# Attention of layer 3: score products on 64-row halves of the array, stacks loaded without stages, causal zeros set after the exponential, maxima over pairs of heads

## What is computed

```python
qkv = jnp.einsum('bsm,qhkm->qbhsk', x, w_qkv)          # x: layer-normed input
scores = jnp.einsum('bhqk,bhsk->bhqs', Q, K) / jnp.sqrt(jnp.float32(d_k))
scores = jnp.where(causal, -jnp.inf, scores)            # causal: key after query
probs = jax.nn.softmax(scores, axis=-1)
attn = jnp.einsum('bhqs,bhsk->bhqk', probs, V)          # then w_o, layer norm, x = x + ...
```

## Time and profile before

| | |
|---|---|
| median of 3 runs | 1885.78 us (1883.0 to 1894.48) |
| profiled execution | 1892.21 us, of which the span is 1890.4 us |
| layers 1 and 2, to the barrier near 395 us | 395 us |
| layer 3, from there to the barrier near 1190 us | about 795 us |
| layer 4 with its weight loads | about 700 us |
| mean granted TensorE clock | 0.932 of 2.4 GHz |
| busy: PE, DVE, ACT, POOL | 1648.1, 1080.8, 914.3, 279.1 us |

### The profile page before, as it was taken

The page is one execution under the profiler, slowest core; times in us unless marked ns, Lnnn a source line. Parts: engine busy times, 40 slices in busy tenths (PEclk is TensorE's granted clock), DMA queues, the critical chain, the costliest instruction groups (busy, mean ns, idle before and its releaser), DMA issues.

```text
span 1890.4 us, 25225 instructions
## 1 busy us (share of the span) xinstructions
PE 1648.1 (87%) x9170; PEld 1214.8 (64%) x9170; DVE 1080.8 (57%) x3056; ACT 914.3 (48%) x1750; POOL 279.1 (15%) x729
## 2 busy tenths in 40 slices
PE   6998857625998999899989998399999999999996
PEld 5877755523555555555545554288888888888885
DVE  5867548855975787678767872234333343434332
ACT  3454425622465666566656666134343443434432
POOL 2123221230110121012101201200101011010101
PEclk9999977866799999999999999599999999999998
DMA  3001112225422531363054400540000000000000
GB/s 117 12 34 36 44 40 89 76 76 66 54 27 35 80 68 25 43 83 69 13 61 54 82 11 2 174 143 1 1 23 23 1 23 1 23 16 8 12 1 23
DMA packets 52869, 83.39 MB, mean 44 GB/s; under 512 B 6784, under 2 KB 41216, under 8 KB 49856
## 3 DMA queue, kind: packets, MB, share of 16 engines
q1 hardware_dynamic: 46416, 68.72, 18.7%
q0 software_dynamic: 5840, 12.33, 2.1%
q10 hardware_dynamic: 480, 0.66, 0.3%
HBM read 43.40 MB, written 12.58 MB: 30 GB/s over the span
## 4 chain that ended last, share of the span: by engine, by line
PE 64%; DVE 13%; SPq 6%; ACT 5%; DMA 5%; issue 4%; POOL 1%; POOLq 1%; ACTq 1%; DVEq 0%
PE psum L812 24%; PE psum L542 12%; PE psum L786 6%; SPq L1748 6%; PE psum L727 5%; PE psum L682 5%; PE psum L709 4%; PE psum L825 3%; PE psum L546 2%; DVE mxs L1416 2%; ACT pr L1027 2%; DMA stage_k<-k_lo 2%; DMA shared_xn<-x_stream 1%; PE psum L712 1%; DVE stat_out L1140 1%
## 5 line engine op out<-in xcount | busy, mean ns | idle before, releaser
L812 PE MATMUL psum<-fh_hi,fWh 128*128 128x512 f32 x1024 | 399.0, 390 | 0.0
L812 PE MATMUL psum<-fh_lo,fWh 128*128 128x512 f32 x1024 | 398.4, 389 | 0.0
L1027 ACT ACTIVATE pr<-psum 128x512 f32<-128x512 f32 (+3 forms) x768 | 344.4, 495 | 106.8 <-PE psum L712 76.4
L1176 DVE TENSOR_TENSOR fh_lo<-fraw,fh_hi 128x512 fp32r<-128x512 f32 x192 | 132.9, 692 | 380.3 <-ACT fh_hi L1090 335.6
L682 PE MATMUL psum<-Ks,Qs 128*128 128x512 f32 (+3 forms) x768 | 311.7, 423 | 33.6 <-DVE mxs L1416 13.2
L709 PE MATMUL psum<-Qs,Ks 128*128 128x512 f32 (+3 forms) x768 | 265.2, 361 | 29.4 <-ACT pr L1027 28.4
L1086 ACT ACTIVATE fraw<-psum,fsch 128x512 f32<-128x512 f32 x128 | 86.5, 676 | 301.9 <-PE psum L812 301.9
L812 PEld LDWEIGHTS psum<-fh_hi,fWh 128*128 128x128 f32 x1024 | 192.2, 188 | 39.7
L812 PEld LDWEIGHTS psum<-fh_lo,fWh 128*128 128x128 f32 x1024 | 192.3, 188 | 39.6
L682 PEld LDWEIGHTS psum<-Ks,Qs 128*128 128x128 f32 x768 | 156.5, 204 | 91.0 <-DVE mxs L1423 31.6
L709 PEld LDWEIGHTS psum<-Qs,Ks 128*128 128x128 f32 x768 | 147.2, 192 | 56.7 <-ACT pr L1027 47.6
(11 more groups left out here) (228 smaller groups left out, 2893.5 us busy)
## 6 DMA issues: line engine op xcount, KB each, us to landing
stage_q<-q_hi SPq DMA_DIRECT2D x60, 128.0 KB, 5.5
stage_k<-k_hi SPq DMA_DIRECT2D x60, 128.0 KB, 5.3
xr<-x_stream SPq DMA_DIRECT2D x9, 512.0 KB, 6.0
x<-in_x SPq DMA_DIRECT2D x8, 512.0 KB, 8.0
raw<-in_h1T SPq DMA_DIRECT2D x16, 256.0 KB, 2.6
raw<-in_h2T SPq DMA_DIRECT2D x16, 256.0 KB, 2.7
x_stream<-x SPq DMA_DIRECT2D x8, 512.0 KB, 3.2
shared_xn<-x_stream SPq DMA_DIRECT2D x8, 512.0 KB, 4.5
```

Source lines behind the costliest of these rows:

```text
L812: m = e.matmul(psum[:, ring4.bank[u], :], f.W[name][:, c, oc * P:(oc + 1) * P], h[:, c, :], start=(c, k) == (0, 0), stop=(c, k) == last)
L1027: e.activation(pr[:, 2 * (s % 2) + pair, side, 0:width], psum[:, (3, 4, 5)[nr % 3], 0:width], ACT.Exp, scale=SC1).then_inc(*mark("act", "s ...
L1176: return e.tensor_tensor(dst, src, plain(hi), ALU.subtract).then_inc(*mark("dve", kind))
```

## The change

Eight edits in layer 3, all in one diff:

1. `Ks` has one copy without zeros. `score3` (was `max3`) and `st3` take rows 64·side to 64·side + 48 (50), one half of the array's rows. Within a step a `score3` of one side alternates with an `st3` of the **other** side.
2. On the diagonal blocks of the maxima, a new PE unit `diag3` adds the bf16 triangle (two matmuls a pair of heads) behind all eight products of the step. DVE's custom instruction, `maskw` and its reading of the accumulator go.
3. DVE's `max3` is one reduce for both sides of a pair (two banks in one instruction, 128x2 out of up to 1024), 24 a group instead of 48; `best3` joins the two column halves of queries 512 to 1023.
4. The triangle products L712 of `st3` go; a new POOL unit `mask3` sets zeros in the first 128 columns of the four exponentials (one `affine_select` over 512 elements a row) on the 8 diagonal steps.
5. `pv3` runs two steps behind instead of one, and `pr` has three buffers instead of two.
6. The DMAs of `stack3` write `Qs` and `Ks` themselves. `copy3`, the stages and their memsets go; `NST` is 4. Later groups' `stack3` stand 36 (25 at a new batch) instead of 27 (23) steps ahead.
7. **Banks:** the ring of the loop has two places, `[0, 2]`. A pair's two scores take one place (banks 0 and 1, or 2 and 3), and so does every side unit. `st3` has 4, 5 and 6.
8. The order of `MAXBLOCKS` and some steps in `plan` differ (`val3` of the first half one step earlier, the second half's projection 3 to 4 steps earlier, the output projection 2 later).

```diff
-NST = 3
+NST = 4
...
-    (0, 0), (1, 0), (3, 0), (4, 0), (5, 0), (2, 0), (7, 0), (7, BANK), (6, 0), (6, BANK), (5, BANK), (4, BANK))]
+    (3, 0), (0, 0), (4, 0), (1, 0), (5, 0), (2, 0), (6, 0), (4, BANK), (7, 0), (5, BANK), (7, BANK), (6, BANK))]
...
-            at([s0 - (27 if g % G else 23)], [("stack3", g, None)])
...
+            at([max(s0 - (36 if g % G else 25), -LEAD)], [("stack3", g, None)])
...
-            at([s0 + n for n in (21, 22, 23, 24, 26, 27)], proj(b + 1, 1))
+            at([s0 + n for n in (18, 19, 20, 21, 22, 23)], proj(b + 1, 1))
...
         for pair, side in HEADS:
...
-                units.append(("max3", *divmod(s + LEAD, NS), pair, side))
+            if ahead:
+                products.append(("score3", *ahead, pair, side))
             if 0 <= s < total:
-                units.append(("st3", s, pair, side))
...
+                products.append(("st3", s, pair, 1 - side if ahead else side))
+        if ahead:
+            i, k0, width = MAXBLOCKS[ahead[1]]
+            diagonal = k0 + width == (i + 1) * P
+            units += [(kind, *ahead, pair) for kind in (("diag3", "max3") if diagonal else ("max3",)) for pair in range(2)]
...
+            units.append(("mask3", s))
+        if 0 <= s - 2 < total:
+            units.append(("pv3", s - 2))
...
-                ring3.banks, ring3.turn = [2], 0
+                ring3.banks, ring3.turn = [0, 2], 0
...
-            Ks = [sb(ph, f"Ks{i}", [P, 2, 2, S], f32r) for i in range(NST)]
-            stage = [sb(ph, f"stage_{m}", [P, 2, S]) for m in "qk"]
...
+            Ks = [sb(ph, f"Ks{i}", [P, 2, S], f32r) for i in range(NST)]
...
+            def score3(g, n, pair, side):
+                u, (i, k0, width), r = ("max3", g, n, pair), MAXBLOCKS[n], rows_of(side, KR)
+                w.wait_ge(*stacked(g))
+                w.wait_ge(*back(ring3, u))
+                e.matmul(psum[:, ring3.bank[u] + side, 0:width], Qs[g % NST][r, pair, i * P:(i + 1) * P],
...
+            def diag3(g, n, pair):
+                bank, width = ring3.bank["max3", g, n, pair], MAXBLOCKS[n][2]
+                for side in range(2):
+                    m = e.matmul(psum[:, bank + side, width - P:width], ident16[:, :], tri16[:, :], start=False, stop=True)
+                m.then_inc(*mark("pe", "diag3"))
...
-                if diag:
-                    m = e.matmul(psum[:, bank, 0:P], tri16[:, :], ident16[:, :], start=False, stop=True)
...
-                e.activation(Ks[g % NST][r, side, pair, :], stage[1][r, pair, :], ACT.Copy).then_inc(*mark("act", "copy3"))
...
+                e.tensor_reduce(mxs[:, g % 2, k0 // BANK, :, pair, i], psum[:, bank:bank + 2, 0:width], AX.X,
+                                ALU.max).then_inc(*mark("dve", "max3"))
...
+                e.affine_select(out=blocks, in_=blocks, compare_op=ALU.is_ge, fill=0.0, base=0, pattern=[[0, 2], [0, 2], [1, P]],
+                                channel_multiplier=-1).then_inc(*mark("pool", "mask3"))
```

213 lines of the change are left out of this document (76 added, 137 removed), and 2 rows, old and new, of the table hands_back.

## The result

The changed kernel takes 1984.86 us (median of 4 runs, 1974.34 to 1992.46), the kernel before beside it 1889.44 us: the ratio is 1.0503, with a 95% interval from 1.044 to 1.0566. It is 5% slower, where 1871 us was forecast and 1930 was the upper end of the range. The profiled execution lasts 1990.6 us against 1890.4, at a mean granted clock of 0.869 against 0.932. The layers 1, 2 and 4 are unchanged; the 100 us lie between 450 us and the loop's end at 1277 us (1177 before); what follows the loop is as long as it was.

A forecast was written before the change was run, and what follows sets the result against it. PE looked like the bound, with a bank chain setting a floor of 2.60 us per 512-wide step. 1892.2 - 12 (three batches) - 4 (start copies) + 1 (extra step) = 1877 profiled; median 6.4 lower: 1871 us, range 1792 to 1930.

The forecast's parts named there:

- Rival (c): PE's array streams about half the time; if the loop were granted 0.87, +45 us, 1916, slower; chance 0.20.
- The quiet group: Loop group with hardly a side unit: PE 31.3, DVE 3.0, side units 1.0, together 35.3 us against 35.6.
- a pair's reduce: DVE's maximum for both sides of a pair, not in the trace: between 1.05 and 1.26, taken as 1.15 us.
- the four triangles: `diag3` on 8 diagonal steps a group: 0.48 us for four, between 0.23 and 0.92; 3.8 us a group.
- 3.0 us for DVE: Added to a quiet group where DVE's step outlasts PE's: 0.9 + 0.3, 0.5 and 0.2 among its terms.
- The overlap: Score products on array halves run two at a time; without it, 2.2 us a group more.
- rival (b): The halves don't run at the same time: 2.2 us a group, +35, 1906 us, slower; chance 0.12.
- Side units: Sharing the maxima's two places, a `qk3` delays pair 1's scores: 2.2 instead of 1.61 us, +0.6 each.
- "No change" for the 17 steps ahead of the loop: Lead steps at half clock, DVE busy 32 of 38 us: fewer reduces but longer chains, taken as no change.
- The last two groups: End of the last batch, groups priced at 30.3 and 28.6 us; that batch 136 us, no change.
- The change of form: Tiling-mode changes drain PE; a diagonal step has three, not two: another 0.16 us 128 times would be 20 us, 1891.
- group 6 without its stage wait: Group 6 of the loop: 35.3 against 48.4 us, since two `val3` and the stage's DMA wait are gone.

The follow-up runs named there:

- e12: Changed kernel with triangles behind each pair, side units in the `st3` banks and score products over all 128 rows (two heads summed): 1866.8 us, ratio 0.9877.
- e1: Changed kernel with layer 3's score products over all 128 rows instead of 64-row halves (two heads summed): 1942.8 us, ratio 1.0301.
- e3: Changed kernel with each pair's triangles right behind that pair's two products instead of behind all four: 1901.4 us, ratio 1.009.
- e8: Changed kernel with score products over all 128 rows and triangles right behind each pair (two heads summed): 1890.3 us, ratio 1.0026.
- e10: Changed kernel, still with halves, with triangles right behind each pair and side units in the three `st3` banks: 1887.9 us, ratio 0.9975.

## Why the prediction was wrong

The table puts the runs side by side: rows of the products, place of the triangles, where the side units go, clock for 490 to 1180 us (the loop of e12 ends at 1153; its own clock is 0.99), groups 10 and 5 in us, and the median.

| kernel | rows | triangles | side units | clock | group 10 | group 5 | us |
|---|---|---|---|---|---|---|---|
| changed | half | behind all | places | 0.83 | 36.2 | 55.3 | 1985 |
| e1 | full | behind all | places | 0.98 | 37.5 | 55.2 | 1943 |
| e3 | half | by pairs | places | 0.89 | 33.2 | 49.5 | 1901 |
| e8 | full | by pairs | places | 0.99 | 34.8 | 52.0 | 1890 |
| e10 | half | by pairs | `st3` banks | 0.87 | 32.3 | 48.0 | 1888 |
| e12 | full | by pairs | `st3` banks | 0.97 | 33.9 | 49.2 | 1867 |

**The step that failed is the clock.** The sum priced every product at the full clock and put the clock itself at nothing. Rival (c) named it, with a chance of 0.20 and a price of 45 us at a clock of 0.87. It came at 0.83. Full rows take 42 us off (54 between the loops of the two profiled executions, 768 and 714 us) although they give up the overlap, which is worth 1.3 us in each of the 14 groups with both kinds of products. So the clock costs some 60 to 70 us here, an estimate; on the kernel before the halves cost 72 net. Rival (c)'s rate, 45 us for a fifth of the loop at the low level, fits this: against the kernel before a third more of the profiled loop is at it (mean clock 0.82 against 0.98). What was wrong was how much of the loop would run low, and why. I had derived it from the share of time in which the array streams and from a stretch in which PE idles; the run on rows 0 to 63 shows a clock of 0.50 with PE busy for 98% of the stretch. In these kernels it isn't a risk beside the halves, it is their price. The Trainium skill ("TensorE: Matmul & The Clock Gate", Part 1: The HAM clock gate) ties the clock to how busy the engine has been; that row doesn't agree, if busy is what the profile counts, and the measurement decides.

**The quiet group** was nearly right where the clock is high: 35.3 us forecast, 36.2 measured in group 10 at 0.95. Its terms: a pair's reduce 1.15 forecast, 1.18 measured (2.36 us for two at 512 columns); the four triangles 0.48 forecast, 0.32 from their weight load (1038.57) to that of `pv3` (1038.89). The forecast had 3.0 us for DVE, and the triangles by pairs gave back 3.0 (36.2 to 33.2). That the numbers agree is partly luck: by the forecast's own terms only 1.4 of its 3.0 lay on diagonal steps. So the price of the triangles' place was about twice what the sum had for it, and I left it in without asking what it would do to the clock.

**The overlap** was priced at 2.2 us a group in rival (b), and is worth 1.2 to 1.6 net where the clock is high. Rival (b) itself fell. The Trainium skill ("TensorEngine Tiling (Array Packing)", Key Properties) says that different tiles load and multiply in parallel; the row at 1027.83 agrees.

**Side units** were priced at +0.6 us each. Group 5 came out as forecast but for 2 us (53, against 55.2 at a clock of 1.00), groups 4 and 7 didn't: 48.3 and 41.0 forecast, 54.3 and 45.4 in the run with full rows at 0.97 and 1.00. Over three batches that is some 30 us. Two waits share this, which the run with side units in the `st3` banks and the triangles by pairs both shorten (49.4 and 42.5).

**The start and the end.** "No change" for the 17 steps ahead of the loop was wrong by 7 us (the loop begins at 509.1 us, not 502.3), and the low clock reaches into the loop, 0.62 in a stretch that had 1.00:

```profile
509.10:537.00 27.90, 25.99 (x138) 12.22 (x137) 13.82 (x20) 12.61 (x28) 3.86 (x7) 0.62 0.01 2
```

```profile
509.00:537.00 28.00, 26.92 (x171) 15.12 (x170) 21.40 (x78) 19.04 (x39) 6.22 (x18) 1.00 0.51 59
```

(the same stretch, changed and before). The last two groups were forecast at 59 us and take 77.5 at a clock of 0.67; with full rows (e1) they take 59.6.

So the clock isn't the whole miss. For the run with full rows (e1), 1871 forecast, + 18 for the overlap given up, + 30 for the groups with side units and + 13 for the start (515.2 us there) make 1932, against 1943 measured. Of the 11 us that are left, 5 are the step from the profiled execution to the median, 6.4 us in the forecast and 1.3 there (1944.1 and 1942.8); 6 stay open. The halves put 42 us more on top.

**The change of form.** The prediction weighed the Trainium skill's rule ("TensorEngine Tiling (Array Packing)", Key Properties) that a change of tiling mode drains TensorE, at 20 us for 128 diagonal steps, and left it out of its sum. The trace agrees with the rule for halves against full rows too. The last product of a 512-wide step and the first triangle behind it, with halves and with full rows (e1), both at full clock:

```profile
1034.81 0.49 PE L722 MATMUL psum<-Qs,Ks 50*128 50x512 f32 x1
1035.23 0.28 PE L703 MATMUL psum<-tri,ident 128*128 128x128 bf16 x2
```

```profile
1015.86 0.39 PE L722 MATMUL psum<-Qs,Ks 128*128 128x512 f32 x1
1016.09 0.28 PE L703 MATMUL psum<-tri,ident 128*128 128x128 bf16 x2
```

The starts are 0.42 us apart with halves and 0.23 with full rows: 0.19 us, as much as a change costs in the run with only the maxima in halves. On the 128 diagonal steps, where DVE waits for the triangles, that would be 24 us, so the rule's 20 us did come. In the sum they hardly show, by luck: with this wait in front the four triangles cost 0.19 + 0.32 = 0.51 us, and the forecast had 0.48. The 1.2 to 1.6 us that the overlap is worth a group are what is left after this price.

**What was right**: no waits for the stacks' DMAs; GpSimd's zeros hidden, at 0.64 us each; group 6 without its stage wait, in kind (39.3 us with full rows (e1) at a clock of 1.00, and 48.4 before; the forecast was 35.3, and with halves it is 45.5 at 0.65).

## What to carry to other kernels

Before products are put on a part of the array to run two at a time, ask what the granted clock does: read it for a stretch with such products in your own kernel, for a busy TensorE alone says nothing of it. The form of products should change seldom (0.2 us each time here), and products that share the array as strips should stay together. And a serial chain of two engines with two places (products, triangle, reduce, products) is mended first by moving the small link right behind what it needs; here that was worth 52 us at full clock, where halving the products lost time in every schedule tried.

## What the hardware showed that I had not expected

- TensorE, busy by the profile for 59.78 of 60.9 us, with products on rows 0 to 63 only, was granted 1.2 GHz (0.50) throughout; the same products over 128 rows, busy for 34.27 of 37.5 us, were granted 2.4 GHz (1.00).
- The maxima's products in halves between products of full rows: starts 0.42 us apart instead of 0.23, and a clock of 0.50 in a group in which PE was busy for all of 82.60 us.
- A triangle over the full array starts 0.42 us behind the start of a 512-wide product on half of the rows, and 0.23 behind one on full rows.
- Four value products in four strips of 32 columns take 1.06 us, two of them 1.05.
- In kernels with halves, groups 2 and 6, the same work, take 40.2 us at a clock of 0.85 and 45.5 at 0.65 within one execution, and their runs spread wider (1868 to 1900 us for one kernel) than those with full rows (1864 to 1870).
